# Slot numbers and row numbers taken as integer maxima on VectorE, in a fused vision layer with a routed feed-forward

## The reference

```
h = tokens(x)                                  # 16x16 patch sums, 12 channels, times cw: 64 x 196 x 192
h = h + attention(layernorm(h))                # 12 heads of 16, weights relu(1 + s + s*s/2), normalised
h = h + ffn(layernorm(h))

flat = x.reshape(-1, 192)
probs = softmax(flat @ router_w.T)             # 8 experts
top_w, top_i = top_k(probs, 2); top_w /= top_w.sum(-1, keepdims=True)
for e in range(8):
    w_e = sum(top_w * (top_i == e))
    out += w_e * (gelu(flat @ w1[e] + b1[e]) @ w2[e] + b2[e])
```

## Time and profile before

| | |
|---|---|
| runs of the kernel, us | 1459.25, 1463.55, 1466.14 (median 1463.55) |
| the profiled execution, us | 1466.21, of which the span of its instructions is 1464.2 |
| busy in the span, us | PE 1257.0, PE weight loads 1109.8, DVE 948.2, POOL 721.5, ACT 595.9 |
| mean granted clock of TensorE | 0.916 of full speed |
| steps without tiles | about the first 253 us |
| steps with tiles | to about 1160 us, some 75 us each |
| tail of tiles alone | the rest |

### The profile page before, as it was taken

How to read it: one execution, slowest core, us unless ns; L and a number is a source line. 1 busy time by engine, 2 the same in 40 slices (tenths; PEclk the granted TensorE clock), 3 DMA queues, 4 the chain that set the end, 5 groups by cost and what they waited for, 6 DMA issues and landing times.

```text
span 1464.2 us, 26690 instructions
## 1 busy us (share of the span) xinstructions
PE 1257.0 (86%) x7299; PEld 1109.8 (76%) x7299; DVE 948.2 (65%) x3349; ACT 595.9 (41%) x1127; POOL 721.5 (49%) x557
## 2 busy tenths in 40 slices
PE   4747645898989898989898989898989999999986
PEld 3746535787878697878787878787878888888875
DVE  6777788686867768585858585858592433333444
ACT  0211113353535344444444444445353544454554
POOL 0012433557474747374746565646464664333432
PEclk9975556899999899999999999999998999999999
DMA  8666778667676757676768685858562574544545
GB/s 296 242 241 246 288 243 269 202 188 259 183 251 181 241 170 243 177 248 179 251 179 263 172 271 167 268 154 247 184 147 67 113 205 94 104 109 84 115 108 121
DMA packets 126504, 284.41 MB, mean 194 GB/s; under 512 B 24773, under 2 KB 70454, under 8 KB 126454
## 3 DMA queue, kind: packets, MB, share of 16 engines
q1 hardware_dynamic: 83350, 242.56, 49.0%
q0 software_dynamic: 43104, 41.25, 16.8%
HBM read 228.79 MB, written 54.95 MB: 194 GB/s over the span
## 4 chain that ended last, share of the span: by engine, by line
PE 61%; DVE 25%; issue 6%; ACT 4%; SPq 1%; DMA 1%; DVEq 0%; POOLq 0%; ACTq 0%; POOL 0%
PE ps L979 19%; PE ps L948 19%; DVE red L1050 8%; PE ps L788 5%; PE ps L895 4%; PE ps L884 3%; PE ps L874 2%; PE ps L852 2%; PE ps L919 2%; PE ps L920 2%; DVE hotw L1222 2%; PE ps L862 2%; DVE ridx L1305 2%; DVE stats L1168 1%; DVE topi L1177 1%
## 5 line engine op out<-in xcount | busy, mean ns | idle before, releaser
L979 PE MATMUL ps<-w2a,hid 128*128 x2520 | 458.6, 330 | 12.2 <-ACT hid L713 12.2
L621 POOL DMA_INDIRECT result<-ys,ridx x210 | 330.0, 1571 | 262.6 <-ACT ys L746 180.2
L979 PEld LDWEIGHTS ps<-w2a,hid 128*128 128x128 f32 x2520 | 420.3, 193 | 27.3 <-issue 18.2
L1050 DVE TENSOR_REDUCE red<-xbuf 128x21 f32<-128x672 f32 x448 | 358.5, 843 | 32.1 <-PE ps L852 22.9
L713 ACT ACTIVATE hid<-ps,b1s 128x512 f32<-128x512 f32 (+1 forms) x344 | 223.1, 655 | 347.8 <-PE ps L948 273.9
L610 POOL DMA_INDIRECT rows_d<-rows,sloti x256 | 247.7, 968 | 232.4 <-issue 152.6
L631 POOL TENSOR_TENSOR w1l<-w1r,w1h 128x768 fp32r<-128x768 f32 x74 | 147.9, 2000 | 222.9 <-ACT w1h L725 222.6
L1275 DVE TENSOR_TENSOR xl<-ps,xh 128x512 fp32r<-128x512 f32 (+1 forms) x58 | 37.2, 641 | 279.2 <-ACT xh L732 279.2
L948 PE MATMUL ps<-xh,w1h 128*128 128x512 f32 (+1 forms) x344 | 163.2, 474 | 37.6 <-DVE xb L1287 20.4
L948 PE MATMUL ps<-xl,w1h 128*128 128x512 f32 (+1 forms) x344 | 137.1, 398 | 0.0
L948 PE MATMUL ps<-xh,w1l 128*128 128x512 f32 (+1 forms) x344 | 136.6, 397 | 0.0
(11 more groups left out here) (166 smaller groups left out, 1748.8 us busy)
## 6 DMA issues: line engine op xcount, KB each, us to landing
xbuf<-x SPq DMA_DIRECT2D x224, 672.0 KB, 6.1
w1r<-L_ffn_w SPq DMA_DIRECT2D x118, 384.0 KB, 4.7
xr<-rows_d SPq DMA_DIRECT2D x48, 402.0 KB, 3.3
result<-h1s SPq DMA_DIRECT2D x32, 294.0 KB
w2a<-L_ffn_w SPq DMA_DIRECT2D x8, 576.0 KB, 7.1
rows_d<-rows,sloti POOLq DMA_INDIRECT x256
rows_d<-pad SPq DMA_DIRECT2D x9, 402.0 KB, 4.6
result<-ys,ridx POOLq DMA_INDIRECT x210
```

Of the source, the lines that this page charges most:

```text
L621: pool.indirect_dma_start(out, bass.IndirectOffsetOnAxis(ap=ridx[:, b, n:n + 1], axis=0), ys[:, b, n, :], None, compute_op=ALU.add).then_i ...
L979: last = mm(yout(g, b, n), hid[:, m % 3, cols], w, start=False, stop=m == MC - 1 and n % 2 == 1)
L1050: V.tensor_reduce(red[:, p * SUMS:(p + 1) * SUMS], xbuf[:, k % XSLOTS, h], AX.X, ALU.add).then_inc(s_pooled, 1)
```

## The change

The slots are reduced by a maximum straight into int32, so that the float tensor `slotf`, its wait and the conversion are gone. The row numbers are taken by a TENSOR_REDUCE with maximum over an innermost axis of one element, where a TENSOR_COPY stood. All values are non-negative and each row of eight has one entry that isn't zero, so the maximum is the sum.

```
-        slotf = sb("slotf", [TOK, 2 * NT])
...
-            links = {"step": 45, "pick": 9, "gate": 1}
+            links = {"step": 44, "pick": 9, "gate": 1}
...
-                mark(V.tensor_reduce(slotf[:], hotw[:], AX.X, ALU.add))
-                own(s)
-                V.tensor_copy(sloti[:], slotf[:]).then_inc(s_slots, 1)
+                V.tensor_reduce(sloti[:], hotw[:], AX.X, ALU.max).then_inc(s_slots, 1)
...
-                V.tensor_copy(ridx[:, nb, 0:g].unsqueeze(2),
-                              xr[:, nb, 0:g, ROW - 1:ROW].bitcast(I32)).then_inc(s_idx, 1)
+                V.tensor_reduce(ridx[:, nb, 0:g], xr[:, nb, 0:g, ROW - 1:ROW].bitcast(I32), AX.X,
+                                ALU.max).then_inc(s_idx, 1)
```

## The result

The changed kernel takes 1415.06 us in the median (1412.7 to 1416.99), the kernel before 1464.82 beside it: a ratio of 0.9667, 95% interval 0.9635 to 0.9698, some 50 us faster. The forecast was 1418.

A forecast was written before the change was run, and what follows sets the result against it. Up to S1, DVE's own sequence was taken to set each step's end, with PE behind it; 20.9 + 0.9 + 2.4 + 5.5 + 16.0 = 45.7 us saved gave 1418 us, range 1408 to 1446.

The forecast's parts named there:

- The reductions don't wait: On DVE, TENSOR_REDUCE doesn't wait for POOL's subtraction as copies do; stage I's 2.07 us copy becomes 0.17.
- The clock, 16 us: PE's clock no longer falls behind S1 once its wait is about 0.6 us: 10 x 1.6 = 16.0 us.
- DVE's terms, 20.9 + 0.9 + 2.4 + 5.5 = 29.7 us: DVE time saved: eleven stage I copies 20.9, the first one 0.9, slots 2.4, two long conversions 5.5 us.
- The long conversions, 5.5 us: Two slot conversions on DVE of 2.95 us disappear, saving 2.77 us each, 5.5 in all; bounds 2.8 to 5.5.
- The product `hotw` stays: DVE's two-SBUF-input product before S1 keeps its 2.7 us in about nine steps; nothing was counted for it.
- What is late next: Behind S1, POOL's halves of w1l cost nothing; without ACT's cover, up to 1.8 us a step, some 20.
- rival (3): Another wait, POOL's w1l halves or loads behind the scatters, gives back 15 us: 1449 us; chance 5%.
- (1): DVE's waits go but PE's clock still falls behind S1, 29.7 us saved: 1434 us; chance 27%.
- (2): The reductions on DVE wait too, so only the conversion's 2.4 us are saved: 1461 us; chance 10%.
- (5): Integer maximum takes a slower DVE path, about 2.2 us each, 24 times, costing 48 us: 1482 us; chance 3%.
- (4): More is gained as hotw gets ahead of POOL, nine times 2.4 us: about 1400 us; chance 3%.
- The likeliest case: All DVE and clock terms come true, 45.7 us saved: 1418 us, own range 1410 to 1427; chance 52%.

The follow-up runs named there:

- copy_unread: Changed kernel with one more copy of the same column, into a tensor nobody reads, in front of stage I's reduction: 1452.94 us (ratio 0.9911).
- late_by_two: Changed kernel with two unread reductions that wait for nothing added behind stage I of the third tile: 1452.64 us (ratio 0.9939).
- slots_alone: Changed kernel with stage I's copy put back, so only the slots are reduced by a maximum: 1451.76 us (ratio 0.9902).
- rows_alone: Kernel before with only stage I's copy replaced by a maximum reduction; slots' sum and conversion kept: 1426.95 us (ratio 0.9739).
- pos_in_psum: Changed kernel with pos moved to PSUM, so the product hotw has one SBUF input: 1397.82 us (ratio 0.9569).
- late_by_one: Changed kernel with one unread reduction that waits for nothing added behind stage I of the third tile: 1424.01 us (ratio 0.9738).
- w1l_on_dve: Changed kernel with pos in PSUM and the low halves of w1 from the first tile's list on DVE, not POOL: 1385.59 us (ratio 0.9451).
- slots_only: Changed kernel with stage I's copy put back, run on the chip where the kernel before took 1667 us: 1663.32 us (ratio 0.9979).
- rows_only: Kernel before with only stage I's copy replaced by a maximum reduction, on the chip of 1667 us: 1662.89 us (ratio 0.9984).

## Why the prediction was right, by its own steps

- **The reductions don't wait.** Right: 161 ns at most for stage I, 286 for the slots, and copy_unread shows that it was the copy as such. The reduction of 4 elements took 0.15 us where I had 0.17.
- **The clock, 16 us.** The mechanism is right and was tested by itself (late_by_two), but this is the term that was mis-sized: PE's busy time fell by 25.2 us. I had counted ten falls behind S1, from one step with a short wait. PE's windows before and then after, for the first step with tiles, the ten steps that follow, and all behind the last S1, show where the rest lies:
```profile
262.00:337.00 75.00, 69.03 (x405) 0.95 0.68 205
337.00:1096.00 759.00, 694.12 (x4050) 0.95 0.71 211
1096.00:1464.00 368.00, 340.57 (x1988) 0.98 0.50 113
```
```profile
261.00:331.00 70.00, 66.02 (x405) 1.00 0.69 208
331.00:1049.00 718.00, 674.62 (x4048) 0.98 0.75 223
1049.00:1414.00 365.00, 336.53 (x1991) 0.99 0.51 115
```
  The ten steps give 19.5 us, where nine of my falls make 14.4; the fall at 785 us is in it, and second low stretches that are shorter or gone. The other two stretches give 3.0 and 4.0 (what stands in front of all three takes 1.3 more): there the second low stretch is gone too, which I had not counted. Why it is gone in these two places and stays in most other steps is open.
- **DVE's terms, 20.9 + 0.9 + 2.4 + 5.5 = 29.7 us.** These were too high: the rest of the gain, PE's idle time, is 49.9 - 25.2 = 24.7. By the earlier trace rows and the rows behind the change, S1's waits for `red` are 21.1 us less (27.7 to 6.6) and M4's for `xb` 6.7 less (20.0 to 13.3), but 3.8 of waits for POOL's `w1l` are new. The steps themselves came out: 71.85 us from S1 to S1 in the one shown (71.9 forecast), and five others of the ten within 0.05 of it, the rest between 70.35 and 73.51; 0.74 us of waiting before S1 (0.6 forecast). One long copy was overlooked: the maximum of 2195 ns in the earlier trace rows is at 277.88 us, in the middle of the first step with tiles, and not in front of an S1.
- **The long conversions, 5.5 us, within these terms.** With both edits, the two steps took 76.33 and 76.39 us before and take 70.37 and 70.35, so 6.0 each; a usual step gives 3.7 (75.59 - 71.86), which leaves 2.3 for the conversion where I had 2.77. The 8 us that I expected of slots_alone were too few for another reason: without the conversion's wait the copy isn't late either, and that is counted under stage I. Of its 13.2 us in the span, 2.9 lie behind the last S1 (10.35 earlier there, 1086.25 for 1096.60), which is again the clock: both low stretches behind that S1 are gone.
- **Stage I and the clock alone.** rows_alone gives 38.3 against 37.8 (20.9 + 0.9 + 16). The match is in part luck, since one of the two long conversions went as well.
- **The product `hotw` stays.** Right: 2.7 us in nine steps still.
- **What is late next.** I had costed POOL's halves of `w1l` at nothing. They now hold PE up three times, 3.8 us in all (2.0 at most). That is rival (3) in small, and outweighed by the clock.
- **Rivals.** (1) is ruled out by the windows and by S1's 1.28 us, (2) by the durations, (5) by 0.15 us for an integer maximum. (4) did not happen with this change; pos_in_psum made it happen.
- **The range.** The likeliest case's own range, 1410 to 1427, doesn't come out of the bounds that I named: they give 1416 (0.2 and 1.2 us more gained) to 1431 (1.6, 1.2, 2.7 and 8 us less). The measured 1415 lies just outside them, on the side of more gain.

The net is 49.8 us measured against 45.7 forecast. The sum is nearer than its parts, 16 for 25.2 and 29.7 for 24.7; that they made up for each other is luck.

## What to carry to other kernels

In this kernel a DVE instruction whose longest duration was ten times its median (2195 and 166 ns) was a wait that the profile lists under no wait. The way to find its reason was to look at what POOL did at that moment. The copy, the conversion and the two-input operations on SBUF waited for POOL's subtraction of two SBUF tensors; the reductions, and the product with one operand in PSUM, did not. So where a chain that others wait for stands beside such a POOL instruction, these forms are worth trying; other POOL arithmetic was not tried. And a wait of PE that was shortened by 2 us was worth 3.7 a step here, since it had been long enough to bring the clock down.

## What the runs showed of the hardware that wasn't expected

- *Order and duration.* The copy is recorded 0.2 us before POOL's subtraction and still ends behind it, in the kernel before and in copy_unread. "Whoever issues first gets the shared pair for the whole instruction", says the Trainium skill's page "SBUF — State Buffer" in the section "Who interferes with whom"; the trace records starts and not issues, and the order of the recorded starts does not tell who gets it. In each of these cases POOL was issuing a scatter when the copy started. Small instructions beside a scatter are lengthened too, but by far less: where only another scatter follows, three instructions of the changed kernel that start 0.54 to 0.71 us into a scatter of 1105.34 all end 1.03 to 1.05 us into it.
```profile
1105.88 0.49 DVE L1202 TENSOR_SCALAR ids<-ids 98x8 f32<-98x8 f32 x1
1105.97 0.41 DVE L1204 TENSOR_SCALAR gk<-th 98x8 f32<-98x8 f32 x1
1106.05 0.34 DVE L1205 TENSOR_SCALAR gk<-th 98x8 f32<-98x8 f32 x1
```
  A copy into `ridx` at 884.52 in the kernel before, 0.82 us into a scatter, took 0.20 us. So the 2 us are the subtraction's; that the scatter in front of it holds the copy up until the subtraction takes over would fit, but was not tested.
- *Waiting and the clock.* In this kernel the clock held behind S1 after waits of 1.73 to 1.75 us (late_by_one) and went to the 1.2 GHz level after waits of 2.66 to 2.75. It also fell some 15 to 18 us behind S1, in fewer steps of w1l_on_dve (5 of 11) than of the changed kernel (9 of 11). In the changed kernel's step of 405.04 PE had stood idle for 0.87 and 0.99 us in the 9 us before that fall, waiting for ACT both times; what decides on it was not tested.
- *The chip of 1667 us.* There a step took 85 to 92 us. At the beginning of steps small DVE instructions stood 0.5 to 1.9 us apart with no engine of the program as the reason, and PE's matmuls 1.0 to 1.4 us apart. From the timeline of slots_only on that chip:
```profile
480.65 0.17 DVE L1114 TENSOR_TENSOR newton<-rstd 98x8 f32<-98x8 f32 x1 [1.24 <-DVE rstd L1119]
482.74 0.17 DVE L1116 SCALAR_TENSOR_TENSOR newton<-newton,var 98x8 f32<-98x8 f32 x1 [1.92 <-issue]
483.45 0.17 DVE L1119 SCALAR_TENSOR_TENSOR rstd<-newton,rstd 98x8 f32<-98x8 f32 x1 [0.55 <-DVE newton L1116]
```
  What the engines waited for there is open. On that chip each edit alone gained 0.2%, though in rows_only S1's wait was 0.74 us as it should be in the step looked at. The gains told in this document are those of the chips on which the kernel before takes some 1465 us.
